# One Trainium2 core, two cross-attentions around a Mamba2 block: the written-out first and last groups in another order on all five engines

## What is computed

```python
q = relu(queries @ Wq + bq); k = relu(keys @ Wk + bk); v = relu(values @ Wv + bv)   # 16 heads
a = softmax(where(mask, q k^T / sqrt(dh), 1e-9)); x = layernorm(a v + queries) * gamma + beta
...
z, xBC, dt = split(rms(x) @ in_proj_w)           # 512, 768 and 8 columns
xBC = silu(conv4(xBC)); xh, Bm, Cm = split(xBC)  # causal, 4 taps
h = h * exp(dt * A) + dt * xh * Bm; y = h . Cm   # for each time step
x = x + rms((y + D_skip * xh) * silu(z)) @ out_proj_w
...
x = x + softmax(LN(x) Wq (enc Wk)^T / sqrt(dh)) (enc Wv) @ Wo   # 8 heads
```

## Time and profile before

| what | value |
|---|---|
| three runs | 1328.54, 1330.46, 1331.92 us |
| median | 1330.46 us |
| the profiled execution | 1328.69 us |
| its span (first to last instruction) | 1326.9 us |
| PE busy | 1294.4 us, 98% of the span |
| DVE busy | 1203.0 us, 91% |
| ACT busy | 1132.5 us, 85% |
| POOL busy | 939.2 us, 71% |
| granted TensorE clock | 1.00 in every stretch read |

### The profile page before, as it was taken

One profiled execution on the slowest core, in us unless ns is written; L12 is line 12 of the kernel. 1 busy time (PEld: TensorE's weight loads), 2 busy tenths in 40 slices (PEclk: granted clock), 3 DMA queues, 4 the chain that ended last, 5 costly groups with the idle time before them and its releaser, 6 DMA issues.

```text
span 1326.9 us, 43638 instructions
## 1 busy us (share of the span) xinstructions
PE 1294.4 (98%) x15742; PEld 1151.7 (87%) x15742; DVE 1203.0 (91%) x3036; ACT 1132.5 (85%) x3407; POOL 939.2 (71%) x1209
## 2 busy tenths in 40 slices
...
GB/s 205 73 39 36 70 78 78 46 64 56 69 77 78 48 67 51 69 77 78 70 45 63 58 75 77 77 39 68 59 70 78 77 66 50 53 50 58 50 57 25
DMA packets 41284, 87.02 MB, mean 66 GB/s; under 512 B 5744, under 2 KB 10992, under 8 KB 41072
## 3 DMA queue, kind: packets, MB, share of 16 engines
...
q10 hardware_dynamic: 864, 0.43, 0.1%
...
## 4 chain that ended last, share of the span: by engine, by line
PE 88%; DVE 4%; ACT 4%; issue 2%; DMA 1%; POOL 1%; SPq 0%; ACTq 0%; DVEq 0%
PE bank L320 26%; PE bank L431 10%; PE bank L582 6%; PE bank L421 5%; PE bank L386 5%; PE bank L563 5%; PE bank L445 5%; PE bank L598 4%; PE bank L703 4%; PE bank L365 3%; PE bank L638 3%; PE bank L659 3%; PE bank L688 2%; PE bank L487 2%; PE bank L425 1%
## 5 line engine op out<-in xcount | busy, mean ns | idle before, releaser
L987 DVE SCALAR_TENSOR_TENSOR ACC<-bank,cw,ACC 128x250 f32<-128x250 f32 (+2 forms) x576 | 264.3, 463 | 5.3 <-ACT ACC L1551 2.5
L320 PE MATMUL bank<-xnT,wnl 128*128 128x256 f32 x640 | 199.8, 312 | 3.0 <-DVE XC L1000 1.7
L1638 ACT ACTIVATE PC<-bank,stc 128x128 f32<-128x128 f32 x512 | 183.0, 390 | 7.6 <-DVE stc L1099 4.2
L320 PE MATMUL bank<-xnL,wnh 128*128 128x256 f32 x640 | 178.8, 279 | 0.0
L320 PE MATMUL bank<-xnT,wnh 128*128 128x256 f32 x640 | 178.4, 279 | 0.0
L834 DVE TENSOR_REDUCE sta<-bank 128x4 f32<-128x512 f32 x256 | 164.0, 675 | 8.1 <-PE bank L386 8.1
L1011 DVE TENSOR_TENSOR_SCAN L<-DB,id 128x1024 f32<-128x1024 f32 x64 | 148.2, 2315 | 1.0 <-DMA DB<-dec_scratch 1.0
L320 PEld LDWEIGHTS bank<-xnT,wnl 128*128 128x128 f32 x640 | 120.4, 188 | 25.3 <-issue 17.1
L1453 ACT ACTIVATE PTA<-bank 128x512 f32<-128x512 f32 x256 | 133.4, 628 | 6.9 <-PE bank L425 3.3
L1950 POOL TENSOR_TENSOR PC<-PC,stc 128x512 f32<-128x512 f32 x128 | 132.0, 1041 | 10.2 <-DVE stc L1106 10.2
L320 PEld LDWEIGHTS bank<-xnL,wnh 128*128 128x128 f32 x640 | 120.9, 189 | 0.0
...
## 6 DMA issues: line engine op xcount, KB each, us to landing
...
```

The costliest lines, as they stand in the source:

```text
L320: mm = e.matmul(t[:, c0:c0 + T], wt[:, k, m:m + 128], x[:, k, :], start=(n == 0), stop=(n == 5))
L987: e.scalar_tensor_tensor(out=w, in0=t[:, 0:T].rearrange("p (b t) -> p b t", b=NB)[:, :, 0:125 + k], scalar=cw[:, c, k:k + 1], in1=w, op0=A ...
L1638: op = e.activation(PC[n % 4][:, p, :], t[:, p * 128:(p + 1) * 128], ACT.Exp, bias=stc[g % 4][:, 4 * i + p:4 * i + p + 1], accum_out=stc[g ...
```

## The change

The lists of the prologue and the epilogue are written anew on all five engines, in another order; the loop is as it was, and the same steps are done with the same operations. `unread` becomes a step of its own that first waits until the bank it names is free. There are 195 such matmuls instead of 118: 99 instead of 95 in the prologue, 96 instead of 23 in the epilogue. PE's program has 77 matmuls more; no other engine has an instruction more or less.

```diff
-            def unread(t, n):
+            def unread(name, i, g, n):
+                t, free = bank(name, i, g)
+                if free:
+                    e.wait_ge(*free)
                 for _ in range(n):
                     e.matmul(t[:, 256:512], onesr[:, :], wqh[:, 0, :], start=True, stop=True)
...
-                        if (g, b) == (1, 1):
-                            unread(t, 10)
...
-                    if (g, b) == (0, 0):
-                        t, free = bank("sA", 7, 2)
-                        e.wait_ge(*free)
-                        unread(t, 24)
...
```

SP's list, prologue:

```diff
-            load_x(0); load_c(0); load_m(0); load_x(1); load_t(0); load_c(1); load_m(1); load_m(2); load_x(2); load_c(2)
-            load_x(3); load_x(4); load_t(1); load_c(3); dec_out(0); dec_in(0, 0); load_m(3); dec_in(0, 1); load_m(4)
...
+            load_x(1); load_m(0); load_c(1); load_t(0); load_x(2); load_m(1); load_m(2); load_c(2); load_c(3)
+            load_m(3); load_x(3); load_t(1); load_x(4); load_m(4); dec_out(0); dec_in(0, 0); load_t(2); dec_in(0, 1)
+            load_u(0); dec_out(1); load_c(4); dec_in(1, 0); dec_in(1, 1); load_u(1); load_t(3); load_x(5)
...
```

PE's list, the part from group 1's transposed scores to its dt, and the last lines of the epilogue:

```diff
-            dp(0, 0); tn(1, 0); cp(0, 1); cp(0, 2); z(0, 0); cp(0, 3); cp(0, 4); sT(1, 0); bd(0, 0); cp(0, 5); av(1, 0)
-            av(1, 1); av(1, 2); av(1, 3); tn(1, 1); k(2, 1); ot(1, 0); z(0, 1); sT(1, 1); bx(0, 0); av(1, 4); av(1, 5)
-            av(1, 6); av(1, 7); ot(1, 1); q(3, 0); q(3, 1); sA(2, 0); bx(0, 1); gm(0, 0); sA(2, 1); y(0, 0); v(3, 0)
-            nt(1, 0); gm(0, 1); k(3, 0); dp(1, 0); cp(1, 0); y(0, 1); cp(1, 1); o(0, 0); cp(1, 2); z(1, 0); cp(1, 3)
...
+            sT(1, 0); bd(0, 0); cp(0, 5); av(1, 0); av(1, 1); av(1, 2); av(1, 3); k(2, 1); tn(1, 1); ot(1, 0)
+            z(0, 1); sT(1, 1); unread("sA", 0, 2, 6); bx(0, 0); av(1, 4); av(1, 5); av(1, 6); av(1, 7); sA(2, 0)
+            ot(1, 1); q(3, 0); q(3, 1); k(3, 0); gm(0, 0); sA(2, 1); bx(0, 1); y(0, 0); v(3, 0)
+            unread("gm", 1, 0, 7); nt(1, 0); gm(0, 1); unread("dp", 0, 1, 13); dp(1, 0); y(0, 1); cp(1, 0); cp(1, 1)
+            o(0, 0); tn(2, 0); z(1, 0); cp(1, 2); cp(1, 3); o(0, 1); sT(2, 0); cp(1, 4); bd(1, 0); cp(1, 5)
...
-            o(NG - 1, 1); tC(NG - 2, 0); tC(NG - 2, 1); k1(NG - 1, 0); ht(NG - 1, 0); k1(NG - 1, 1); ht(NG - 1, 1)
-            tC(NG - 2, 2); q1(NG - 1, 0); q1(NG - 1, 1); tC(NG - 2, 3); sC(NG - 1, 0); oC(NG - 2, 0); oC(NG - 2, 1)
-            v1(NG - 1, 0); wp(NG - 2, 0); tC(NG - 1, 0); tC(NG - 1, 1); tC(NG - 1, 2); tC(NG - 1, 3); oC(NG - 1, 0)
-            oC(NG - 1, 1); wp(NG - 1, 0)
...
+            unread("wp", 0, NG - 4, 18); cp(NG - 1, 5); wp(NG - 4, 0); z(NG - 1, 1); tC(NG - 3, 0); tC(NG - 3, 1)
+            bx(NG - 1, 0); gm(NG - 1, 0); k1(NG - 2, 0); k1(NG - 2, 1); unread("y", 0, NG - 1, 8); y(NG - 1, 0)
+            ht(NG - 2, 0); ht(NG - 2, 1); tC(NG - 3, 2); tC(NG - 3, 3); gm(NG - 1, 1); q1(NG - 2, 0); q1(NG - 2, 1)
+            bx(NG - 1, 1); sC(NG - 2, 0); oC(NG - 3, 0); oC(NG - 3, 1); y(NG - 1, 1); unread("o", 1, NG - 1, 9)
+            o(NG - 1, 0); v1(NG - 2, 0); tC(NG - 2, 0); wp(NG - 3, 0); o(NG - 1, 1); unread("tC", 2, NG - 2, 8)
+            tC(NG - 2, 1); tC(NG - 2, 2); k1(NG - 1, 0); k1(NG - 1, 1); ht(NG - 1, 0); unread("tC", 3, NG - 2, 4)
+            ht(NG - 1, 1); tC(NG - 2, 3); q1(NG - 1, 0); q1(NG - 1, 1); unread("sC", 0, NG - 1, 5); sC(NG - 1, 0)
+            oC(NG - 2, 0); oC(NG - 2, 1); unread("v1", 0, NG - 1, 12); wp(NG - 2, 0); tC(NG - 1, 0); v1(NG - 1, 0)
+            tC(NG - 1, 1); tC(NG - 1, 2); unread("tC", 3, NG - 1, 6); tC(NG - 1, 3); oC(NG - 1, 0); oC(NG - 1, 1)
+            wp(NG - 1, 0)
```

More of the change, by code:

```diff
@@ L303, in sync @@
                 store(g)
[L304 to L311, removed]
+            store(NG - 9); dec_out(NG - 6); load_c(NG - 3); dec_in(NG - 6, 0); load_m(NG - 3); load_m(NG - 2)
+            dec_in(NG - 6, 1); load_x(NG - 2); load_u(NG - 6); load_t(NG - 4); load_c(NG - 2); store(NG - 8)
+            dec_out(NG - 5); load_x(NG - 1); dec_in(NG - 5, 0); load_m(NG - 1); dec_in(NG - 5, 1); load_u(NG - 5)
+            dec_out(NG - 4); load_c(NG - 1); load_t(NG - 3); dec_in(NG - 4, 0); dec_in(NG - 4, 1); load_u(NG - 4)
+            load_u(NG - 3); load_t(NG - 2); store(NG - 7); dec_out(NG - 3); dec_in(NG - 3, 0); dec_in(NG - 3, 1)
+            dec_out(NG - 2); store(NG - 6); load_t(NG - 1); load_u(NG - 2); dec_in(NG - 2, 0); dec_in(NG - 2, 1)
+            store(NG - 5); dec_out(NG - 1); load_u(NG - 1); dec_in(NG - 1, 0); dec_in(NG - 1, 1); store(NG - 4)
+            store(NG - 3); store(NG - 2); store(NG - 1)
             e.wait_ge(d_out[0], 16 * (NG // 2))
@@ L460, in nt @@
                 if ok(g):
-                    if g == 1:
-                        t, free = bank("o", 0, 0)
-                        e.wait_ge(*free)
-                        unread(t, 8)
                     t, free = bank("nt", 0, g)
@@ L501, in cp @@
                 if ok(g):
-                    if (g, c) == (0, 0):
-                        t, free = bank("dp", 0, 0)
-                        e.wait_ge(*free)
-                        unread(t, 13)
                     t, free = bank("cp", c, g)
@@ L557, in y @@
                         e.wait_ge(*free)
-                    if (g, b) == (0, 0):
-                        unread(t, 5)
                     e.wait_ge(s_m, ns + 1)
@@ L572, in o @@
                         e.wait_ge(*free)
-                    if (g, b) == (NG - 1, 0):
-                        unread(t, 10)
                     if ns == 0:
@@ L590, in ht @@
                         e.wait_ge(*free)
-                    if g == NG - 1:
-                        unread(t, 9 - 5 * b)
                     e.wait_ge(s_hx, 2 * g + b + 1)
@@ new lines, in vector @@
+            tap(NG - 2, 16); tap(NG - 2, 17); xc(NG - 2, 3); xc(NG - 2, 4); xc(NG - 2, 5); bs(NG - 1, 0)
+            bg(NG - 1, 0); hm(NG - 3, 0); hm(NG - 3, 1); xs(NG - 1, 0); scan(NG - 2, 0); sz(NG - 2, 1)
+            rc(NG - 1, 1); kk1(NG - 3, 0); xo(NG - 1, 1); x2(NG - 1, 0); kk1(NG - 3, 1); bs(NG - 1, 1)
+            bg(NG - 1, 1); lg(NG - 2, 0); xs(NG - 1, 1); x2(NG - 1, 1); yd(NG - 2, 0); scan(NG - 2, 1)
+            mC(NG - 3, 0); mC(NG - 3, 1); nl(NG - 1, 0); nl(NG - 1, 1); lg(NG - 2, 1); d0(NG - 1, 0); d0(NG - 1, 1)
```

530 lines of the change are left out of this document (267 added, 263 removed).

## The result

The changed kernel takes 1322.72 us (median of 5 runs, 1322.32 to 1323.71) against 1329.47 for the kernel before (5 runs): a ratio of 0.9949, 95% interval 0.9937 to 0.9960, or 6.75 us less. Later series of the kernel before, of 27, 21 and 24 runs, have medians of 1330.32, 1330.46 and 1330.59. Against these it is 7.6 to 7.9 us.

A forecast was written before the change was run, and what follows sets the result against it. The prediction took PE, busy for 98% of the span, as the bound, with DVE next. Prologue -4 and epilogue -1 gave -5 us: 1323.7 us profiled, 1325.5 as the median, range 1320 to 1332.

The forecast's parts named there:

- the larger gain: Rival: scans run unhindered and the epilogue's idle goes, -9 us, 1321.5 us; chance 0.17.
- The first group: Start of prologue: first scores 0.8 to 1.5 us later, won back to 1 us of lead at group 0's convolution.
- sA(2, 0): Prologue: group 2's scores start at about 62 us, 5.4 earlier; nt(1, 0) and dp(1, 0) follow; 4 us taken.
- The bound of 5.8: Prologue: most it could gain, from DVE's idle of 5.4 us and the 1 us lead less work in it.
- The 34 products: Unread blocks of 10 and 24 on PE, 1.45 and 3.11 us; the 24 called longer than filling a wait needs.
- The scans: Group 0's two scans on DVE, stretched by POOL operations, 2 x 1.0 us; the stretch was left in.
- SP: Later fetch of the second sequence's decays, landing at 71 to 72 us; cost 0 to 2 us, taken as 0.
- 82 us and on: From 82 to 205 us both engines are full; taken as 0, bounds -1 and +1 us.
- Epilogue: Up to the last scan -1 us, bounds -2.2 and +0.5; tail behind it 0, bounds -1 and +1.
- The slower one: Rival: the 77 added unread products outlast their waits, 9.2 us more work, +4.2 us, 1334.7 us; chance 0.10.
- The eaten lead: Rival: DVE, full from 120 to 150 us, or late DB(0, 1) eats the 4 us lead; 1329.5 us; chance 0.23.
- The other signs: Signs of being right: sA(2, 0) at about 62 us, lg(0, 0) by 68, dp(1, 0) at 77 to 78.

The follow-up runs named there:

- Run e: The changed kernel with the steps up to group 0's first transpose nt(0, 0) in the old order on all engines: 1322.67 us, ratio 0.9945.
- the three moves: The kernel before with only ke(2, 1) on ACT, qm(2, *) on POOL and sA(2, 0) on PE moved earlier, unread products kept: 1331.87 us, ratio 1.0011.
- d: The kernel before without its 118 unread products: 1332.02 us, ratio 1.0015.
- run j: The changed kernel with 10 unread products put back ahead of ot(1, 1) and 24 ahead of gm(0, 0): 1327.36 us, ratio 0.9976.
- run c: The changed kernel without its 195 unread products: 1328.60 us, ratio 0.9984.

## Why the prediction was right, step by step

The forecast was 1325.5 us, 5 below the 1330.46 from which it started. Measured was 1322.72, 7.7 below that and 6.75 below the kernel before run beside it: inside the range. The mechanism is the forecast's own: a lead won in the prologue, carried whole through the loop, and next to nothing in the epilogue. By the number alone the larger gain, 1321.5, lies nearer. The prologue's term was too small, and part of its reasoning wrong.

*The first group.* Forecast: first scores 0.8 to 1.5 us late, 1 us of lead by the convolution. The split cost nothing: it ran at 11.59 us, before the first keys were through. The distance to nt(0, 0) fell by 0.8 us, near the forecast. Run e, without it, is no slower, but its start differs, so what the 0.8 us are worth stays open.

*sA(2, 0).* The size was right: 5.2 us earlier, measured from the first scores, against 5.4. The weight was wrong. "From there nt(1, 0) and dp(1, 0) follow" is the step that failed: with this move alone they don't. What held them was the chain from ot(1, 1) and q(3, *) over ACT and POOL to DVE's statistics, and the change opens it elsewhere: on POOL qm(3, 0) stands behind ga(0, 1) and no longer ahead of xr(1, 1), on ACT qe(3, 0) goes ahead of the split. That these two moves are what the lead needs was not run by itself; shown is that the three without them give nothing.

*The bound of 5.8.* The prologue broke it, with 8.2. Of the four waits of DVE that make up its 5.4 us, the one of 2.08 lies at 35.36 us, outside the stretch, and one of 0.83 ahead of y at 75.84 is left out. The stretch ahead of 60 us was not looked into: there PE waits 1.69 us at 50.95 in the kernel before and still 1.45 with the three moves; in the changed kernel no wait of PE from nt(0, 0) to dp(1, 0) is above 0.5.

*The 34 products.* That the block of 24 ahead of gm(0, 0) outlasts its wait was read rightly, but in the old order little was behind it: 1.3 us with the three moves. Without those moves the blocks were not taken out by themselves; d, without all 118, is slower. Only in the new order would the 34 cost 3.6.

*The scans.* 2 us of stretch were left in; 1.6 of it went, a part of the larger gain's case.

*SP.* DB(0, 1) was asked for at 69.18 us and was there when scan(0, 1) began at 73.92: taken as 0, rightly. *82 us and on.* Taken as 0 with bounds of 1; measured -1.3, a little outside.

Sum for the prologue: 8.2 us in place of 4. In the two profiles only 5.55 of it is seen, since the profiled execution of before had the first keys at full speed. It lay 1.8 us under its median, which fits that, and the sum had carried these 1.8 us over as a constant. That the profiles come so near the forecast is luck: the term was half of what it should have been, and the start hid 2.6 us.

*Epilogue.* Forecast -1 before the last scan and 0 behind it; measured +0.5 and -1.0. That the two come to nearly the same sum is luck too. cp(31, 5) came 0.8 us late against sA(10, 0) and 1.0 against sA(28, 0), worked out were 0.5.

*The rivals.* The slower one named a real price, for run j pays it. In the changed kernel the blocks differ: PE waits behind the one ahead of cp(31, 5), but not behind the one ahead of o(31, 0), and behind one of the two that lie on the chain in the tail it doesn't either. That is one of the signs that the prediction named for being wrong. What these blocks cost is open; run c shows that all of them together save more. The eaten lead falls: DVE at 29.00 of 30 us took it all in.

*The other signs.* sA(2, 0) at 64.95 and lg(0, 0) at 69.61 us missed the places named, 62 and 68, and less the 2.6 us of the start they met them. dp(1, 0) at 77.48 met its place only with those 2.6 us: it came sooner than forecast.

The Trainium skill, "SBUF — State Buffer", section "SBUF: two separate sides", was weighed for the scans: whichever of the two engines starts first blocks the other. The trace agrees from both sides: in the kernel before POOL began at 62.23 us, 0.1 us before the scan, and the scan took 3.33 us; in the changed kernel the scan began at 63.94 us, POOL's operation at 65.13, and that took 2.17 us in place of 1.27.
